# Two key tiles at a time on the TensorE of an attention kernel, with the rows of far values and maxima first, through four row tiles of 32 rows

## The reference, cut to what matters

```python
# x: (B=2, S=2048, D=256), 16 heads of 64 values, all f32
h = layernorm(x)
q, k, v = (h @ w for w in (wq, wk, wv))                  # split into heads
scores = q @ k.T + rel_bias[bucket(key - query)]         # 32 buckets, 16 on each side
o = softmax(scores) @ v
x = x + layernorm(o @ wo)
x = x + layernorm(mixture of 8 dense experts with gelu, top-2 gates per batch)(layernorm(x))
```

## Time and profile before

| | |
|---|---|
| median of 3 runs | 3407.9 us (3405.98 to 3410.67) |
| the profiled execution | 3413.72 us, span 3411.9 us, mean granted clock 0.945 |
| busy: PE, POOL, DVE, ACT | 89%, 67%, 66%, 41% of the span |
| loop of 8 pairs of heads | from about 135 to 3060 us of the span |

### The profile page before, as it was taken

The page is one execution under the profiler, slowest core; times in us unless marked ns, Lnnn a source line. Parts: engine busy times, 40 slices in busy tenths (PEclk is TensorE's granted clock), DMA queues, the critical chain, the costliest instruction groups (busy, mean ns, idle before and its releaser), DMA issues.

```text
span 3411.9 us, 57378 instructions
## 1 busy us (share of the span) xinstructions
PE 3034.7 (89%) x18988; PEld 998.4 (29%) x18988; DVE 2242.1 (66%) x4237; ACT 1392.6 (41%) x1786; POOL 2276.5 (67%) x1033
## 2 busy tenths in 40 slices
PE   3599989999999999998999999999999899983846
PEld 2132322323232323232332323232323232321423
DVE  5666666666666666666766666667666666666676
ACT  2144434443444444443444344444444344442423
POOL 0187877877778777876878777777787787870000
PEclk8699999999999999999999999999999999995968
DMA  6000000000000000000000000000000000002000
GB/s 146 16 1 2 1 17 2 1 1 2 18 1 1 1 18 2 1 1 18 1 1 1 1 17 2 1 1 17 1 2 1 17 2 1 1 1 74 1 25 25
DMA packets 45641, 38.32 MB, mean 11 GB/s; under 512 B 21318, under 2 KB 43846, under 8 KB 45046
## 3 DMA queue, kind: packets, MB, share of 16 engines
q1 hardware_dynamic: 45302, 34.13, 3.8%
HBM read 29.17 MB, written 11.34 MB: 12 GB/s over the span
## 4 chain that ended last, share of the span: by engine, by line
PE 61%; issue 16%; DVE 12%; ACT 3%; POOL 3%; DMA 2%; SPq 2%; DVEq 1%; ACTq 0%; POOLq 0%
PE st L480 20%; PE po L509 20%; PE pre L491 6%; PE st L675 5%; PE pm L448 3%; DVE mpart L928 3%; PE pm L454 3%; POOL acc L420 3%; PE pm L539 2%; DVE st L945 2%; ACT prob L726 2%; DVE pre L925 2%; PE pm L518 1%; DVE eq L890 1%; DMA t_scratch<-w_scratch 1%
## 5 line engine op out<-in xcount | busy, mean ns | idle before, releaser
L420 POOL TENSOR_TENSOR acc<-acc,prob 128x1024 f32<-128x1024 f32 x896 | 2113.2, 2358 | 548.8 <-ACT prob L726 505.4
L726 ACT ACTIVATE prob<-st 128x1024 f32<-128x1024 f32 x1026 | 1024.9, 1022 | 1421.4 <-DVE st L945 1016.7
L928 DVE TENSOR_REDUCE mpart<-pre 128x2 f32<-128x1024 f32 x686 | 840.1, 1225 | 465.7 <-PE pre L491 463.8
L509 PE MATMUL po<-prob,v 128*64 128x512 f32 x4096 | 1128.7, 630 | 0.0
L480 PE MATMUL st<-qk 64*128 64x512 f16 x6156 | 860.2, 386 | 38.9 <-issue 27.0
L925 DVE CUSTOM_DVE_ANT_0 pre<-pre,tab 128x512 f32<-128x512 f32 x718 | 482.7, 714 | 217.4 <-issue 216.4
L491 PE MATMUL pre<-qk 64*128 64x512 f16 x2090 | 408.1, 387 | 113.1 <-DVE mpart L928 68.1
L480 PEld LDWEIGHTS st<-qk 64*128 64x128 f16 x6156 | 219.1, 95 | 757.1 <-issue 322.0
L480 PE MATMUL st<-eq,ek 64*128 64x512 f16 x2052 | 395.2, 382 | 0.0
L509 PEld LDWEIGHTS po<-prob,v 128*64 128x64 f32 x4096 | 204.8, 136 | 429.4 <-issue 371.9
L420 POOL TENSOR_TENSOR acc<-prob 128x1024 f32<-128x1024 f32 x64 | 150.6, 2353 | 175.3 <-ACT prob L726 156.0
(11 more groups left out here) (132 smaller groups left out, 2118.5 us busy)
## 6 DMA issues: line engine op xcount, KB each, us to landing
t_scratch<-w_scratch SPq DMA_DIRECT2D x2, 3072.0 KB
inv_r<-inv SPq DMA_DIRECT2D x260, 1.0 KB, 1.7
y<-x SPq DMA_DIRECT2D x2, 2048.0 KB, 11.6
qk<-x SPq DMA_DIRECT2D x2, 2048.0 KB, 12.5
out<-qk SPq DMA_DIRECT2D x2, 2048.0 KB, 7.5
w<-w_pairs SPq DMA_DIRECT2D x9, 384.0 KB, 4.1
t2f<-t_scratch SPq DMA_DIRECT2D x9, 384.0 KB, 4.7
t<-t_scratch SPq DMA_DIRECT2D x8, 384.0 KB, 3.1
```

Source lines behind the costliest of these rows:

```text
L420: nc.gpsimd.tensor_tensor(acc[g % 2][:, :, :], a, prob[:, n % RING, :, :], ALU.add).then_inc(sum_p, 1)
L509: last = nc.tensor.matmul(po[64 * h:64 * h + 64, :], v[:, g // CHUNKS, j, 64 * h:64 * h + 64], prob[:, n % RING, h, :], start=(s == 0), st ...
L726: nc.scalar.activation(prob[:, n % RING, :, :], st[:, 2 * (n % 2):2 * (n % 2) + 2, :], ACT.Exp).then_inc(exp_done, 1)
L928: nc.vector.reduce_max(mpart[:, c, :, t, kc, 0], pre[:, :, :], AX.X).then_inc(pre_used, 2)
```

## The change

PE, ACT and DVE go through two steps (n even, n and n + 1) in one turn. PE's turn is now: the fourth term of steps n + 2 and n + 3 for both heads, as four matmuls in row tiles of 32 rows that start the four banks of `st`; the first piece; the three other terms of n + 2, then of n + 3; the second piece; the jobs of n; `values` of n and n + 1; the jobs of n + 1. The four first matmuls wait for the exponentials of both steps before. DVE's turn is maximum, band, maximum, band and then the rest of both steps; ACT's is two exponentials and then the rest of both. The rows of `eq` and `ek` now repeat every 32 partitions: head 0 has row tiles 0 and 2, head 1 has 1 and 3. So SP issues four DMAs of maxima for a group where it issued two, and `far_rows` is one instruction on 128 partitions where it was two on 32. The jobs stand at other steps.

```diff
-JOBS = {0: ("proj", 0), 2: ("den", 0), 4: ("proj", 1), 6: ("proj", 2), 8: ("inv", 0), 10: ("y", 0), 11: ("max", 0), 12: ("y", 1),
-        14: ("proj", 3)}
-INV_AT, REST_AT, HIGH_AT, LOW_AT = 5, 7, 9, 9
+JOBS = {1: ("den", 0), 2: ("proj", 0), 4: ("proj", 1), 6: ("proj", 2), 8: ("inv", 0), 11: ("max", 0), 12: ("y", 0), 14: ("y", 1),
+        15: ("proj", 3)}
+INV_AT, REST_AT, HIGH_AT, LOW_AT = 4, 6, 9, 10
@@ max_in (SP)
-                for h in range(2):
-                    sp.dma_start(eq[64 * h + M_ROW:64 * h + M_ROW + 1, g % 2, :]...
+                for k in range(4):
+                    h = k % 2
+                    sp.dma_start(eq[32 * k + M_ROW:32 * k + M_ROW + 1, g % 2, :]...
@@ PE
+            def scores_rows(i, n):
+                for d in range(2):
+                    scores_wait(i, n + d)
+                for d in range(2):
+                    g, s, j = step_of(n + d)
+                    for h in range(2):
+                        k = 2 * d + h
+                        nc.tensor.matmul(st[:, k, :], ek[32 * k:32 * k + 32, variant(g % CHUNKS, j), :],
+                                         eq[32 * k:32 * k + 32, g % 2, :], start=True, stop=False)
...
-                         (kl[b][:, keys], qh[b][:, queries]), (ek[:, variant(c, j), :], eq[:, g % 2, :])]
...
-                                                start=(r == 0), stop=(r == len(terms) - 1))
+                                                start=False, stop=(r == len(terms) - 1))
...
+                for n in range(0, STEPS, 2):
+                    scores_rows(i, n + 2)
+                    next_piece(n)
+                    for m in (n + 2, n + 3):
+                        scores(m)
+                    next_piece(n + 1)
+                    before = jobs(n, before)
+                    values(i, n)
+                    values(i, n + 1)
+                    before = jobs(n + 1, before)
@@ ACT
+                for n in range(0, STEPS, 2):
+                    for m in (n + 2, n + 3):
+                        bands = probs(i, m, bands)
+                    rest(n)
+                    rest(n + 1)
@@ DVE, far_rows
-                for h in range(2):
-                    nc.vector.tensor_scalar(eq[64 * h:64 * h + 32, buf, :]...
+                nc.vector.tensor_scalar(eq[:, buf, :]...
@@ DVE, loop
+                for n in range(0, STEPS, 2):
+                    next_maximum(n)
+                    bands = band(i, n + 2, bands)
+                    next_maximum(n + 1)
+                    bands = band(i, n + 3, bands)
+                    rest(n)
+                    rest(n + 1)
```

More of the change, by code:

```diff
@@ L18 @@
 KC = S // 512
+M_ROW = 2 * QT
 BAND = 3 * 128
@@ L25 @@
 BUCKET_FROM = [0, 1, 2, 3, 4, 5, 6, 7, 8, 12, 16, 23, 32, 46, 64, 91]
-M_ROW = 32
 SEL = 11 + TT * TT // 4
-ROWS = SEL + 128
+ODD = SEL + 128 + 1
+ROWS = ODD + 1
 W_UNIT = 64.0
@@ L114, in shape_tables @@
     rows[:, 10] = (QT <= r) & (r < 2 * QT)
+    for h in range(2):
+        rows[:, ODD - 1 + h] = np.arange(128) // 32 % 2 == h
     for i in range(TT):
@@ L118, in shape_tables @@
     for n in range(4):
-        rows[n, SEL:] = (np.arange(128) // 64 == n % 2) / INV_UNIT
+        rows[n, SEL:SEL + 128] = (np.arange(128) // 64 == n % 2) / INV_UNIT
     return onehot, rows, np.eye(128, dtype=np.float32)
@@ L475, in scores @@
                 keys, queries = slice(128 * j, 128 * j + 128), slice(QC * c, QC * c + QC)
-                terms = [(kh[b][:, keys], qh[b][:, queries]), (kh[b][:, keys], ql[b][:, queries]),
-                         (kl[b][:, keys], qh[b][:, queries]), (ek[:, variant(c, j), :], eq[:, g % 2, :])]
+                terms = [(kh[b][:, keys], qh[b][:, queries]), (kh[b][:, keys], ql[b][:, queries]), (kl[b][:, keys], qh[b][:, queries])]
                 for r, (w, t) in enumerate(terms):
@@ L493, in piece, with maxima @@
                 last.then_inc(pre_ready, 1)
-            def maxima(G):
+            def maxima(G, far):
+                pe.wait_ge(far_set, far)
                 pe.wait_ge(m_col, G + 1)
@@ L581, in _ @@
                 piece(0, 0, u)
-            maxima(0)
+            maxima(0, 1)
             pe.wait_ge(v_a, 4)
+            scores_rows(0, 0)
             for n in range(2):
-                scores_wait(0, n)
                 scores(n)
@@ L589, in _, with next_piece @@
             pe.wait_ge(set_pool, 2)
-            pe.wait_ge(set_v, 14)
+            pe.wait_ge(set_v, 16)
             with pe.Fori(0, PAIRS) as i:
                 before = (SLOTS - 1, jobs_of(SLOTS - 1)[-1])
-                for n in range(STEPS):
+                def next_piece(n):
                     g, s, _ = step_of(n)
-                    G = i * SLOTS + g
-                    scores_wait(i, n + 2)
-                    scores(n + 2)
                     ahead, u = piece_at(s)
@@ L603, in _, with jobs @@
                     piece(i * SLOTS + to, to % SLOTS, u)
-                    values(i, n)
+                def jobs(n, before):
+                    g, s, _ = step_of(n)
+                    G = i * SLOTS + g
                     for at, kind, k in jobs_of(g):
@@ L624, in _ @@
                         else:
-                            maxima(G + 1)
-            pe.wait_ge(m_row, G_ALL + 1)
+                            maxima(G + 1, 2 * i + (3 if g == SLOTS - 1 else 2))
+                    return before
+                for n in range(0, STEPS, 2):
[8 more added lines that the diff above has]
+                    before = jobs(n + 1, before)
+            pe.wait_ge(y_add, G_ALL * YJ + 1)
             denominators(G_ALL, 0)
@@ L769, in _, with rest @@
                 bands = 0
-                for n in range(STEPS):
+                def rest(n):
                     g, s, _ = step_of(n)
                     G = i * SLOTS + g
-                    bands = probs(i, n + 2, bands)
                     if s == TT - 1:
@@ L886, in far_rows @@
             def far_rows(pair, buf):
[L889 to L892 removed]
+                nc.vector.tensor_scalar(eq[:, buf, :].rearrange("p (t q) -> p t q", q=128),
+                                        rowc[:, 0:QT].unsqueeze(2).broadcast_to((128, QT, 128)),
+                                        fpair[:, 1, bass.ds(pair, 1)], None, ALU.mult).then_inc(far_set, 1)
             def pair_table(pair, k):
@@ L995, in _ @@
                 nc.vector.tensor_copy(farv[:, 1, to:to + heads], far[:, 2, 0:heads]).then_inc(set_v, 1)
+            dve.wait_ge(set_v, 10)
+            nc.vector.tensor_scalar(fpair[:, 0, :], farv[:, 0, :].rearrange("p (n h) -> p n h", h=2)[:, :, 1], rowc[:, ODD:ODD + 1], None,
+                                    ALU.mult).then_inc(set_v, 1)
+            dve.wait_ge(set_v, 11)
+            nc.vector.scalar_tensor_tensor(fpair[:, 1, :], farv[:, 0, :].rearrange("p (n h) -> p n h", h=2)[:, :, 0], rowc[:, ODD - 1:ODD],
+                                           fpair[:, 0, :], ALU.mult, ALU.add).then_inc(set_v, 1)
             nc.vector.tensor_copy(ek[:, :, :], rowc[:, QT:QT + 5].unsqueeze(2).broadcast_to((128, 5, 128))).then_inc(set_v, 1)
             nc.vector.memset(eq[:, :, :], 0.0).then_inc(set_v, 1)
-            nc.vector.tensor_copy(sel[:, :], rowc[0:4, SEL:ROWS]).then_inc(set_v, 1)
+            nc.vector.tensor_copy(sel[:, :], rowc[0:4, SEL:SEL + 128]).then_inc(set_v, 1)
             nc.vector.memset(tab[:, :, 0:3, :], 0.0).then_inc(set_v, 1)
@@ L1016, in _ @@
             dve.nop().then_inc(pre_used, 2)
+            dve.nop().then_inc(y_add, 1)
             dve.nop().then_inc(band_in, 1)
@@ L1025, in _, with next_maximum @@
                 bands = 0
-                for n in range(STEPS):
+                def next_maximum(n):
                     g, s, _ = step_of(n)
@@ L1035, in _, with rest @@
                     piece_max(G + ahead, (g + ahead) % SLOTS, u)
-                    bands = band(i, n + 2, bands)
+                def rest(n):
+                    g, s, _ = step_of(n)
+                    G = i * SLOTS + g
                     if s == 4 and g == 0:
@@ L1044, in _ @@
                         low_weights(i + 1)
-                    if g == 0 and s == WO_AT + 1:
+                    if g == 1 and s == 1:
                         low_wo(i)
```

23 lines of the change are left out of this document (11 added, 12 removed).

## The result

The changed kernel takes 3483.61 us (median of 4 runs, 3481.79 to 3489.36) against 3409.28 beside it: ratio 1.0219, interval 1.02 to 1.0238. It is 74 us slower; the forecast was 59, so 3467 in a range of 3385 to 3535.

The account below looks back on a forecast made before the run. PE was taken to bound the kernel, its savings outweighed by new waits for DVE and ACT. Profiled 3413.7 plus 59 us (7.4 a head pair) gave 3473, a median of 3467; range 3385 to 3535 for 8 in 10.

Parts of the forecast that it names:

- PE's bound and the plain turn: The loop goes at PE's pace; PE's work for a turn of two steps falls from 4.40 to 4.31 us.
- The pass for four tiles: Start of PE's turn: four row matmuls stream as two do, in 0.22 us; 0.44 if two by two.
- the change of tiling: On PE after the row matmuls, going from 32 to 64 rows: taken at 0.09 us, between 0 and 0.11.
- The piece's wait: PE's second piece waits for DVE's first maximum, one buffer `pre`: 1.78 us piece to piece, nearly 0.3 waiting every turn.
- The wait in its place: Row matmuls wait for both exponentials; a second-tile band queues behind both maxima, ending the exponential at 4.92 us plus its width.
- DVE's rest: Low part of step 15's projection holds DVE to 1.36 us instead of 0.80, next turn's chain 0.56 later (c = 1, 2).
- Projections of v: Turns with a projection and no wait last 4.31 + 1.40 = 5.71 us; v has no low part.
- Groups: Turns summed by group: c = 1 +1.6 us, c = 2 +1.4, c = 0 +0.7; 7.4 a head pair, 59 for eight.
- c = 3: Groups without projections: new waits overlap existing waits for DVE; between 0 and +3 us, taken as 0.
- The stall of 4.5 at the loop's start: PE's stall of 4.5 us at the loop's start was to stay unchanged.
- the far rows: One DVE instruction for two saves 1.9 us twice a head pair: at best 30 us, at worst 0, taken as 0.
- PE's savings win: Rival: DVE and ACT don't bind, turns are 4.31 us plus jobs, -1.2 a group, 3331 us in all; chance 0.17.

Follow-up runs that it names:

- two_row_tiles: Changed kernel with the second tile's far rows on row tiles 0 and 1, so the four matmuls go two by two: 3574.21 us, ratio 1.0483.
- band_and_job_first: Changed kernel with DVE's order maximum, band, band, maximum and the jobs of even steps ahead of the second piece: 3336.86 us, ratio 0.9782.
- job_before_piece: Changed kernel with the jobs of even steps ahead of the second piece rather than behind it: 3529.48 us, ratio 1.035.
- band_first: Changed kernel with DVE's order in a turn as maximum, band, band, maximum: 3377.2 us, ratio 0.9904.
- split_rows: Changed kernel with two row matmuls ahead of the first piece, two ahead of the second tile's scores, each pair awaiting one exponential: 3433.87 us, ratio 1.0066.
- no_last_low: Changed kernel without the low parts of the fourth projection of q and of k in the loop: 3473.0 us, ratio 1.0181.
- far_rows_twice: Changed kernel with the DVE instruction that writes the far values into eq issued twice in a row: 3500.67 us, ratio 1.0264.
- and_max_at_13: Changed kernel with band, band before second maximum, even jobs before second piece, and max job moved from step 11 to 13: 3717.42 us, ratio 1.0896.

## Why the prediction was right, and where it was off

1. **PE's bound and the plain turn.** Right: 4.30 for 4.31. The pass for four tiles (0.22) and the change of tiling (0.09; measured 0.10) held, both shown by two_row_tiles. The drain that the Trainium skill (TensorEngine Tiling (Array Packing), Key Properties) gives for a changed tiling mode fits that 0.10 for 32 to 64 rows. By the estimate from the Trainium skill (TensorE: Matmul & The Clock Gate, Measured speedup vs the span model) the pass would have been 0.29; 0.32 less 0.10 leaves 0.22.
2. **The piece's wait.** Right in place and size for plain maxima. It is hidden at the price of a change of tiling only once the band doesn't queue behind it (band_and_job_first against job_before_piece).
3. **The wait in its place.** Right: shown by band_first and split_rows. Mis-sized at turn 10: 5.61 computed, 5.95 and 6.11 measured. The two small reductions of the maxima (0.22 and 0.19) stand between the first and second maximum there, and the first has a bias, so the second starts at 2.84 of the turn, not 2.58; and the next turn starts 0.06 after the exponential's end. I left these out of the sum.
4. **DVE's rest.** The hold of the first maximum is as computed; the low part's share of it is 0.33 a turn, the rest is the wait for the high part (no_last_low). In c = 2, turn 0 at g = 2 was 0.36 longer than computed; a second maximum there started 0.87 after its piece, where 0.49 is usual, and why is open.
5. **Projections of v** were taken at 1.40; turns 2 and 6 of c = 2 have 5.86, so 0.15 more than those of c = 1. In the kernel before the difference is 0.05 (5.84 for 5.79) and with the job ahead of the piece 0.05 (5.58 for 5.53), so most of it belongs to the place of the job; why is open.
6. **Groups.** Changes by group, the mean over the first seven head pairs, against the forecast: c = 1, +2.34 and +2.36 for 1.6; c = 2, +2.81 and +3.05 for 1.4; g = 4, +1.73 for 0.7; c = 3, g = 3: +0.14 for 0. So the regular groups were under-priced by 0.7 to 1.6 each, 6 us a head pair.
7. **The rest.** Here are the failed steps. One is "The stall of 4.5 at the loop's start and the tables stay." The stall fell to 1.2 to 2.2. The granted clock in the 3 us behind it, 0.50 at all seven loop starts before, is below 1.00 at only two of them now. From the turns on both sides of the loop's end this is some 30 us in all, an estimate, and the cause is open. The other is the far rows, which I took at 0 with 30 us at best, and which are worth some 38 (far_rows_twice). The 1.9 that I took for one is a mean with those ahead of the loop; in the loop the median is 2.45, and a piece waited behind them. The page before hints at it: four slices of the loop are at 8 tenths for PE, not one, and all four hold far rows of a g = 7. So g = 0 changes by -0.64 and g = 7 by -2.95 where I had +0.7 and 0: some 4 us a head pair the other way. The errors cancel in part, and that the total came out nearer than its terms, 8.8 a head pair for 7.4, is luck.
8. **c = 3.** The bet that new waits overlap old ones failed, though the sum at g = 3 came out by luck. Turn 2 there is 8.16 for 6.93, so the new wait (1.2 by the forecast's own turns) came on top of the low weights; the same turn is 4.30 in band_first. Turn 8 gives back 2.7 for another reason: the operands of inv arrive before PE asks now. At g = 7 the turns without far rows and loop end grew by 3.3 in sum, the upper end of my 0 to +3, and item 7's two terms hid it.
9. **Rivals.** The first (PE's savings win, 3331) was refuted for this order. With DVE's order changed the times are near its own, 3337 and 3297, but not by its sum of 1.2 less in every group. In band_and_job_first the groups with projections last 43.2 to 44.9, apart from g = 6 with its tables, where they lasted 44.0 to 47.1. The two groups without projections fall from 44.7 and 46.9 to 39.4 and 41.9, at g = 7 with the gain of far rows and loop end. That is 10.3 us together, and a whole head pair gains 10.1. I had put its condition right, a chain shorter than 4.31 plus the job, but not asked which order would meet it.

## What to carry to other kernels

When two steps are merged into one turn, write down for each engine what now stands ahead of the operation that frees the shared buffer; what another engine waits for goes ahead of what only must be done some time. A saving on the bounding engine is paid out only if its next wait has at least that much slack, and here 1.7 to 1.9 us of a group with projections hung on the place of one DVE line (band_first). Fixing a wait that is visible but behind another made things worse (job_before_piece), and better once the first was gone: test such edits together as well as alone. An instruction's mean over the whole program can hide what it costs in one place: read its duration where another engine waits for it.

## What the runs showed of the hardware that was not expected

- Four matmuls of 32 rows each on four row tiles and four banks start within 0.01 us of each other and take one pass: 0.32 to the next matmul, change of tiling included, against 0.54 with two tiles.
- PE stands idle at a loop's end: 2.6 to 4.8 us with about 1.6 queued behind its last wait (before), 1.2 to 2.2 with 2.8 (changed kernel), but also 2.7 to 3.3 with 2.6 (far_rows_twice). So what is queued is not all that sets it.
- The write of far values takes 0.49 us on 128 partitions and 0.47 on 32 with POOL idle. Started while POOL sums, it ends 0.28 after POOL's instruction: 1.12 to 1.55 in the changed kernel, 2.45 to 2.60 in the one before, but 0.47 where it starts 0.07 ahead of POOL's. The low weights do the same: 0.96 with POOL idle, otherwise they end 0.81 after POOL's instruction, at 2.80 (before), 2.56 (changed kernel) or 1.40 (band_first). A maximum beside the same POOL instructions keeps its 1.23.
- SP needed 2.50 us to issue four small DMAs, and from the start of the copy to the use of their data 4.04 us passed (and_max_at_13).
